# Grouped attention: the probabilities times values product in three terms of rounded and low parts, with x parked in DRAM

## The reference, cut to what matters

```
h   = layernorm(x) then rmsnorm, scaled by ln1          # 4 x 256 x 256
q   = rope(h @ Wq)     32 heads of 128                    # 4 key/value heads,
k   = rope(h @ Wk)      4 heads of 128                    # each for 8 query heads
v   = h @ Wv            4 heads of 128
p   = softmax(q k^T / sqrt(128), causal)
res = layernorm(x) + (p v) @ Wo
```

## Time and profile before

| what | value |
|---|---|
| median of 3 runs | 1535.27 us (1535.23 to 1543.98) |
| the profiled execution | 1537.94 us, span 1536.2 us |
| PE busy | 1342.8 us (87%) |
| PE weight loads | 987.4 us (64%) |
| DVE busy | 961.9 us (63%) |
| ACT busy | 792.4 us (52%) |
| POOL busy | 617.7 us (40%) |
| stage of the change | 716 to 1233 us of the span |
| rounds of its loop | 750 to 1232 us |

### The profile page before, as it was taken

How to read it: one execution, slowest core, us unless ns; L and a number is a source line. 1 busy time by engine, 2 the same in 40 slices (tenths; PEclk the granted TensorE clock), 3 DMA queues, 4 the chain that set the end, 5 groups by cost and what they waited for, 6 DMA issues and landing times. The chain is left out here.

```text
span 1536.2 us, 23871 instructions
## 1 busy us (share of the span) xinstructions
PE 1342.8 (87%) x8621; PEld 987.4 (64%) x8621; DVE 961.9 (63%) x1625; ACT 792.4 (52%) x1590; POOL 617.7 (40%) x550
## 2 busy tenths in 40 slices
PE   5788678899799579886789999999999869999998
PEld 4564455644388434433557777776777658888887
DVE  4763754558755587873677777877787554333443
ACT  2455104345532246664567777777877544445442
POOL 5110001101054511211566666666676445555553
PEclk8999779989999678996899999999999979999999
DMA  2000400020000100002000000000000023233231
GB/s 70 1 1 2 121 3 0 4 101 0 1 1 1 38 1 2 2 2 81 7 14 15 15 25 19 15 22 22 15 22 8 8 87 121 96 119 110 105 119 51
DMA packets 29492, 55.58 MB, mean 36 GB/s; under 512 B 6506, under 2 KB 16170, under 8 KB 29204
## 3 DMA queue, kind: packets, MB, share of 16 engines
q1 hardware_dynamic: 29396, 54.30, 11.0%
HBM read 52.98 MB, written 1.21 MB: 35 GB/s over the span
## 5 line engine op out<-in xcount | busy, mean ns | idle before, releaser
L2606 DVE TENSOR_TENSOR e_act<-e_gated,ps 128x512 f32<-128x512 f32 x66 | 45.4, 688 | 158.1 <-POOL e_gated L2411 158.1
L1839 POOL TENSOR_TENSOR a_raw<-a_prod 128x512 f32<-128x512 f32 x72 | 98.3, 1366 | 51.7 <-DVE a_prod L2243 51.7
L1844 POOL TENSOR_TENSOR a_q_low<-a_raw,a_q_high 128x512 fp32r<-128x512 f32 x64 | 82.8, 1294 | 87.2 <-ACT a_q_high L2103 87.2
L2240 DVE TENSOR_TENSOR a_prod<-ps,a_rot 128x512 f32<-128x512 f32 x72 | 49.7, 691 | 93.9 <-PE ps L1888 93.7
L2411 POOL TENSOR_TENSOR e_gated<-e_gate,e_wb 128x512 f32<-128x512 f32 x66 | 85.2, 1292 | 49.8 <-ACT e_gate L2532 44.5
L1848 POOL TENSOR_TENSOR a_o_low<-a_o,a_o_high 128x512 fp32r<-128x512 f32 x64 | 82.9, 1295 | 41.7 <-ACT a_o_high L2154 39.7
L2111 ACT ACTIVATE a_shift<-ident,a_nmax 128x128 bf16<-128x128 f32 x256 | 81.9, 390 | 32.3 <-DVE a_nmax L2252 32.0
L2402 POOL TENSOR_TENSOR e_we_low<-e_we,e_we_high 128x768 fp32r<-128x768 f32 x33 | 60.8, 1842 | 89.5 <-ACT e_we_high L2537 85.5
L1606 DVE SCALAR_TENSOR_TENSOR m_acc<-ps,m_conv_w,m_acc 128x1020 f32<-128x1020 f32 (+2 forms) x60 | 76.0, 1275 | 31.3 <-ACT m_acc L1526 29.9
L1360 PE MATMUL ps<-m_ln_T,m_win 128*128 128x512 f32 x192 | 88.8, 618 | 4.2 <-DMA m_win<-in_m_winT 3.5
L601 DVE TENSOR_REDUCE x_nmax<-ps 128x2 bf16<-128x512 f32 x128 | 82.5, 689 | 11.2 <-PE ps L371 10.9
(11 more groups left out here) (431 smaller groups left out, 4271.2 us busy)
## 6 DMA issues: line engine op xcount, KB each, us to landing
e_wb<-token_weights SPq DMA_DIRECT2D x32, 512.0 KB, 3.9
e_we<-in_experts SPq DMA_DIRECT2D x33, 384.0 KB, 3.1
a_wq<-in_a_wq SPq DMA_DIRECT2D x16, 256.0 KB, 2.7
a_wo<-in_a_wo SPq DMA_DIRECT2D x16, 256.0 KB, 2.8
m_win<-in_m_winT SPq DMA_DIRECT2D x2, 1024.0 KB, 8.8
nf_pickU<-in_nf_pickU SPq DMA_DIRECT2D x2, 768.0 KB
nf_raw<-in_ffn_w SPq DMA_DIRECT2D x3, 352.0 KB
x<-in_x SPq DMA_DIRECT2D x4, 256.0 KB, 6.6
```

What stands on the lines that cost most here:

```text
L1839: e.tensor_tensor(raw[:, i % 2, :], prod[:, i % 2, 0, :], prod[:, i % 2, 1, :], ALU.add).then_inc(s_raw, 1)
L1844: e.tensor_tensor(low_part, raw[:, i % 2, :], high_part.bitcast(F32), ALU.subtract).then_inc(s_xl, 1)
```

## The change

v is kept as a rounded part `vH` and a low part `vL`, the probabilities as `pH` and `pL`. Their product is vH pH + vH pL + vL pH, three fp32r matmuls for each one in fp32. The new work of a round: ACT `prob_high(n-1)` behind `exps(n-1)` rounds 128x768 probabilities in one instruction; POOL `prob_low` subtracts the long part, 128x512, behind `low`; DVE `prob_low` subtracts the short part, 128x256, behind `rotate` and ahead of `split`. In the prologue DVE makes eight `v_low` (128x512, one operand in PSUM) among the rotations.

To make room, buffers share memory: `raw` becomes the first half of `prod` (so `rotate(i)` waits until `low(i-2)` is done, where it waited for `add(i-2)`), the q pieces have three slots of 512 columns, the probabilities three (four before) beside four of pH and pL, `o_high` three (four before), wk, wv, the parts of wv, `pick32` and `normed` lie in buffers that are used later, and `inv`, `inv_high` and `o` lie in `core.x`. For that x is stored to DRAM (1 MB, the issue comes behind `odd` on SP) and DVE waits for that ahead of the loop; in the next stage SP loads it back behind the bias and ahead of experts 1 to 3, and POOL waits for it ahead of its x + res.

```diff
+        probT = sb("probT", [P, 3, 3 * S])
+        room = core.x[:].rearrange("p t d -> p (t d)")
+        inv, invH = (room[:, z:z + 2 * S].rearrange("p (r n) -> p r n", r=2) for z in (0, 2 * S))
+        o = room[:, 4 * S:8 * S].rearrange("p (r n) -> p r n", r=2)
+        pH, pL = sb("prob_high", [P, 4, 3 * S], F32R), sb("prob_low", [P, 4, 3 * S], F32R)
-        v = sb("v", [P, NT, NKV * P])
+        vH, vL = sb("v_high", [P, NT, NKV * P], F32R), sb("v_low", [P, NT, NKV * P], F32R)
         prod = sb("prod", [P, 2, 2, BANK])
-        raw = sb("raw", [P, 2, BANK])
+        raw = prod[:, :, 0, :]
...
             e.dma_start(odd[:], d["odd"]).then_inc(s_pick, 16)
+            e.dma_start(d["x_saved"], core.x[:].rearrange("p t d -> p (t d)")).then_inc(s_saved, 16)
...
+        def prob_low(e, n, part, done):
+            e.wait_ge(s_ph, n + 1)
+            e.tensor_tensor(pL[:, n % 4, part], probT[:, n % 3, part], pH[:, n % 4, part].bitcast(F32),
+                            ALU.subtract).then_inc(done, 1)
...  (POOL's loop)
                 for i in of_step.get(n - 1, ()):
                     low(e, i)
+                if 0 <= n - 1 < N:
+                    prob_low(e, n - 1, slice(0, 2 * S), s_pll)
...  (TensorE: values_of waits for v_low, values)
                 if t >= 4:
-                    e.wait_ge(s_vc, t - 3)
+                    e.wait_ge(s_vl, t - 3)
...
+                e.wait_ge(s_pll, s + 1)
+                e.wait_ge(s_pls, s + 1)
                 if s >= 1:
                     e.wait_ge(s_o, s)
-                e.matmul(out, v[:, 2 * b, g * P:(g + 1) * P],
-                         probT[:, s % 4, 0:2 * S].rearrange("p (h q) -> p h q", h=2), start=True, stop=False)
-                e.matmul(out[:, :, P:S], v[:, 2 * b + 1, g * P:(g + 1) * P],
-                         probT[:, s % 4, 2 * S:3 * S].rearrange("p (h q) -> p h q", h=2),
-                         start=False, stop=True).then_inc(s_av, 1)
+                for k, o, part in ((0, out, slice(0, 2 * S)), (1, out[:, :, P:S], slice(2 * S, 3 * S))):
+                    for i, (w, x) in enumerate(((vH, pH), (vH, pL), (vL, pH))):
+                        mm = e.matmul(o, w[:, 2 * b + k, group], heads(x[:, s % 4, part]), start=(k == i == 0),
+                                      stop=(k == 1 and i == 2))
+                mm.then_inc(s_av, 1)
...  (ACT's loop, behind exps(n - 1) and ahead of copy_spread)
+            def prob_high(n):
+                e.wait_ge(s_ex, 2 * n + 2)
+                if n >= 4:
+                    e.wait_ge(s_av, n - 3)
+                e.activation(pH[:, n % 4, :], probT[:, n % 3, :], ACT.Copy).then_inc(s_ph, 1)
...  (DVE)
+            def v_low(t):
+                e.wait_ge(s_vc, t + 1)
+                e.tensor_tensor(vL[:, t, :], ps[:, (P2_LONG, AV, SPREAD, OUT)[t % 4], :], vH[:, t, :].bitcast(F32),
+                                ALU.subtract).then_inc(s_vl, 1)
...
             def rotate(i):
                 e.wait_ge(s_pc, i + 1)
                 if i >= 2:
-                    e.wait_ge(s_raw, i - 1)
+                    e.wait_ge(s_xh, i - 1)
+                    e.wait_ge(s_xl, i - 1)
...
-            for i in range(1, FIRST):
-                rotate(i)
+            rotate(1)
+            rotate(2)
+            for t in range(4):
+                v_low(t)
+            rotate(3)
+            rotate(4)
+            for t in range(4, 6):
+                v_low(t)
+            rotate(5)
+            for t in range(6, 8):
+                v_low(t)
...  (DVE's loop)
                 for i in of_step.get(n, ()):
                     rotate(i)
+                if 0 <= n - 1 < N:
+                    prob_low(e, n - 1, slice(2 * S, 3 * S), s_pls)
                 if n % 2 and 0 <= n - 3 < N:
                     split((n - 3) // 2)
...  (next stage, SP and POOL)
             e.dma_start(bias[:], d["expert_bias"].partition_broadcast(P)).then_inc(s_w, 16)
+            e.dma_start(core.x[:].rearrange("p t d -> p (t d)"), d["x_saved"]).then_inc(s_back, 16)
...
             weights_low(0, 0)
+            e.wait_ge(s_back, 16)
             e.tensor_tensor(core.x[:], core.x[:], res[:], ALU.add).then_inc(s_xr, 1)
```

More of the change, by code:

```diff
@@ L1730, in stage_attention_1 @@
         mv, rstd1, rstd2, ahead = core.mv, core.rstd, core.rstd2, Ahead(core, "a1", res, "rms")
-        normed = sb("normed", [P, 4, D])
         hH, hL = sb("h_high", [P, KD, T], F32R), sb("h_low", [P, KD, T], F32R)
         over = sb("over", [P, 2, 2 * S])
-        o = sb("o", [P, 2, 2 * S])
-        wk, wv = over, o
-        wkH, wvH = sb("wk_high", [P, KD, NKV * P], F32R), sb("wv_high", [P, KD, NKV * P], F32R)
+        probT = sb("probT", [P, 3, 3 * S])
+        begin = probT[:].rearrange("p r n -> p (r n)")
+        wk, wv = (begin[:, z:z + KD * NKV * P].rearrange("p (k n) -> p k n", k=KD) for z in (0, 1024))
+        room = core.x[:].rearrange("p t d -> p (t d)")
+        inv, invH = (room[:, z:z + 2 * S].rearrange("p (r n) -> p r n", r=2) for z in (0, 2 * S))
+        invH = invH.bitcast(F32R)
+        o = room[:, 4 * S:8 * S].rearrange("p (r n) -> p r n", r=2)
+        pH, pL = sb("prob_high", [P, 4, 3 * S], F32R), sb("prob_low", [P, 4, 3 * S], F32R)
+        early = pH[:].rearrange("p r n -> p (r n)")
+        wvH, wvL = (early[:, z:z + KD * NKV * P].rearrange("p (k n) -> p k n", k=KD) for z in (1024, 2048))
+        wkH = sb("wk_high", [P, KD, NKV * P], F32R)
         wq, wqH = sb("wq", [P, 2, 2, KD, P]), sb("wq_high", [P, 2, 2, KD, P], F32R)
         wo, woH = sb("wo", [P, 2, 2, D]), sb("wo_high", [P, 2, 2, D], F32R)
-        wkL, wvL = sb("wk_low", [P, KD, NKV * P], F32R), sb("wv_low", [P, KD, NKV * P], F32R)
+        wkL = sb("wk_low", [P, KD, NKV * P], F32R)
         wqL, woL = sb("wq_low", [P, 2, 2, KD, P], F32R), sb("wo_low", [P, 2, 2, D], F32R)
@@ L1743, in stage_attention_1 @@
         ones = sb("ones", [P, 32])
-        pick32, pick = sb("pick32", [P, 4, P]), sb("pick", [P, 4, P], F32R)
+        pick32, pick = over[:, 0].rearrange("p (c n) -> p c n", c=4), sb("pick", [P, 4, P], F32R)
         odd = sb("odd", [P, 1])
@@ L1771, in stage_attention_1 @@
         s_p2, s_ex = sem("scores"), sem("probs")
+        s_ph, s_pll, s_pls = sem("probs_high"), sem("probs_low_long"), sem("probs_low_short")
+        s_vl, s_saved = sem("v_low"), sem("x_saved")
         s_sum, s_inv, s_ih, s_is = sem("sums"), sem("inverses"), sem("inverses_high"), sem("inverses_split")
@@ L1816, in target @@
             _, p, half, j = what
-            a = slice(half * BANK, (half + 1) * BANK)
-            return qH[:, p % 2, j, a], qL[:, p % 2, j, a], 2 * (B * (p - 2) + 2 * half + 2)
+            at = 2 * p + half
+            return qH[:, at % 3, j, :], qL[:, at % 3, j, :], 2 * (B * ((at - 3) // 2) + 2 * ((at - 3) % 2) + 2)
         def const_low(e, n):
@@ L1947, in first_scores @@
                 e.wait_ge(s_m1, n + 1)
-                a = b * S
+                a, at, z = b * S, (2 * p + b // 2) % 3, b % 2 * S
                 long = ps[:, P1_LONG, :].rearrange("p (h k) -> p h k", h=2)
                 for j in range(2):
-                    e.matmul(long[:, j, :], qH[:, p % 2, j, a + P:a + S], kH[:, p // 4 % 2, a:a + S],
+                    e.matmul(long[:, j, :], qH[:, at, j, z + P:z + S], kH[:, p // 4 % 2, a:a + S],
                              start=False, stop=True, skip_group_check=True)
@@ L1954, in first_scores @@
                 for j in range(2):
-                    e.matmul(short[:, j, :], qH[:, p % 2, j, a:a + P], kH[:, p // 4 % 2, a:a + P],
+                    e.matmul(short[:, j, :], qH[:, at, j, z:z + P], kH[:, p // 4 % 2, a:a + P],
                              start=(j == 0), stop=False, skip_group_check=True)
@@ L1970, in scores @@
                 keys = [w[:, g, a:a + P] for w in (kH, kL)]
-                both = [w[:, p % 2, :, a:a + S] for w in (qH, qL)]
+                both = [w[:, at, :, z:z + S] for w in (qH, qL)]
                 e.wait_ge(s_m2, 2 * n + 1)
@@ L1978, in scores @@
                 keys = [w[:, g, a + P:a + S] for w in (kH, kL)]
-                both = [w[:, p % 2, :, a + P:a + S] for w in (qH, qL)]
+                both = [w[:, at, :, z + P:z + S] for w in (qH, qL)]
                 e.wait_ge(s_m2, 2 * n + 2)
@@ L2095, in v_copy @@
                 e.wait_ge(s_v, t + 1)
-                e.activation(v[:, t, :], ps[:, (P2_LONG, AV, SPREAD, OUT)[t % 4], :], ACT.Copy).then_inc(s_vc, 1)
+                e.activation(vH[:, t, :], ps[:, (P2_LONG, AV, SPREAD, OUT)[t % 4], :], ACT.Copy).then_inc(s_vc, 1)
             def high(i):
@@ L2130, in exps @@
                 e.wait_ge(s_p2, 2 * n + 1)
-                if n >= 4:
-                    e.wait_ge(s_av, n - 3)
-                e.activation(probT[:, n % 4, 0:2 * S], ps[:, P2_LONG, :], ACT.Exp).then_inc(s_ex, 1)
+                if n >= 3:
+                    e.wait_ge(s_pll, n - 2)
+                    e.wait_ge(s_pls, n - 2)
+                    e.wait_ge(s_sum, (n - 3) // 2 + 1)
```

(6 more changed lines are left out.)

24 lines of the change are left out of this document (13 added, 11 removed).

## The result

The changed kernel takes **1607.65 us** (median of 4 runs, 1601.09 to 1613.08); the kernel before took 1536.48 on the same chip (1535.23 to 1543.98). The ratio is 1.045, 95% interval 1.0399 to 1.0501. The forecast was 1590, its range 1546 to 1625, its sign slower. The profiled execution took 1612.2 (span 1610.4), 74.3 more than the one before.

The account below looks back on a forecast made before the run. TensorE sets the pace now, DVE just behind; after the change the chain through DVE and ACT, plus the port, binds. 34 + 16 + 1 + 7 - 3 = +55 on 1537.94 gives 1593, 1590 as median; range 1546 to 1625.

Parts of the forecast that it names:

- its sign slower: Whole kernel: slower by over 1%, chance 0.79; within 1% 0.16, faster 0.05.
- 34 + 16 + 1 + 7 - 3 = 55: Collision in 24 pairs 34 us, six k-piece pairs 16, two last pairs 1, prologue 7, less 3 for splits already held.
- the gain: TensorE's values in the loop: 1.03 us instead of 1.29, 0.26 a round, 17 us over 64, counted inside pair times.
- the mask among the rivals: Rival: ACT's late second mask holds short scores, or POOL first; 1634 at most; above 1625, clock included, 0.08.
- its chain: Loop, divide to next divide through DVE and ACT, with prob_high and prob_low: 6.40 us in even rounds, 6.80 in odd.
- The collision, the step of +1.4 a pair: Odd rounds: split held 1.05 us by POOL's prob_low; pair 14.9, 34 us over 24 pairs; case 1568 to 1625, chance 0.63.
- two branches: Odd rounds: DVE first, split held, pair +1.4 (chosen); or POOL first, prob_low held too, pair +2.7.
- k pieces, +2.7: Six loop pairs with a k piece: rotate waits 1.6 for low, +2.7 each, 16 us in all, range 10 to 26.
- The prologue, +7: Ahead of the loop: eight v_low on DVE make the loop's first piece late, +7 us, between 5 and 10.
- Costed at nothing: x's transfer to DRAM and back, the slots of q, probabilities and o_high, and values' new waits: 0 us.
- The clock, a rival: Clock falls as TensorE idles more: +45 for a tenth of the loop, 1635; above 1625, either cause, chance 0.08.
- TensorE's gain survives, a rival: Loop pair 13.02: 1525 with prologue paid, chance 0.08; 1518 with it hidden, 0.04.

Follow-up runs that it names:

- fill: Changed kernel plus four more fp32r matmuls of 512 columns in even rounds while TensorE waits for split: 1592.84 us, ratio 1.0274; repeated on another chip 1596.47 us, 1.0381.
- after_again: The changed kernel itself, nothing altered, run once more in the third set of runs: 1607.07 us, ratio 1.0451 to the kernel before.
- no_lows: Changed kernel with both prob_low (DVE's and POOL's) left out, prob_high kept, TensorE's work the same: 1563.85 us, ratio 1.020 to the kernel before.
- terms_only: Changed kernel without prob_high and both prob_low; only the three matmuls, v_low and shared buffers are left: 1538.88 us, ratio 1.0033 to the kernel before.
- dve_early: Changed kernel, all arithmetic kept, DVE's prob_low moved a round later and ahead of the rotation: 1555.84 us, ratio 1.006 to the kernel before.
- no_v_low: Changed kernel without the prologue's eight v_low, rounded v standing in the third term: 1593.88 us, ratio 1.0375 to the kernel before.

## Why the prediction was right, and where not

**Sign and size.** The sum was 34 + 16 + 1 + 7 - 3 = 55. With the clock held up (`fill`), the loop is 497.4 against 449.2: +48.2, where the terms gave 34 + 16 + 1 - 3 = 48. The prologue is +8.3 to the first `maxima` where 7 was put. The clock makes +14.2 in the profiled execution (511.6 - 497.4), and 8.3 + 48.2 + 14.2 - 0.2 = 70.5. The forecast for this execution was 1593, and it took 1612: 14 of the 19 are the clock, for which the sum had no term, 4 the stages ahead, 1 the prologue.

**TensorE.** `values` is now 1.06 in the array (from 1022.70, its first slot in the next even round, to the piece at 1023.76), forecast 1.03. That the gain would be inside the pair times held for TensorE's own rounds: in `after_again` `values` start at 924.24, 931.29 and 939.67, so 7.05 for the one with `sums` (forecast 7.06) and 8.38 for the other (7.85).

**ACT.** 836 ns, as forecast. Its place costs more than was seen: 0.77 a pair by `no_lows` against `terms_only`, through the second mask and through `inverse_high`, which both come behind it. The forecast had the mask among the rivals only, and `inverse_high` nowhere: its chain followed the input of `prob_low`, not that of `split`, though the earlier trace rows had shown the case: there `split` waited 0.72 for `inverse_high` and then took 1.53. Here both lie beneath the larger delay of the odd rounds and show where that is taken away (`dve_early`).

**The collision, the step of +1.4 a pair.** Its size was nearly right at full clock: 15.13 against the 13.54 from which it was worked out, +1.59, and with the give-back, which lies in the mean of 13.70, +1.43. That is in good part luck. The forecast had two branches and chose one. If `prob_high` comes last, `prob_low` runs free and only `split` is held: 14.9 forecast, 14.5 measured, in five of the 20 pairs (seven with the extra matmuls). If the rotation comes last, POOL is first and both are held: 13.54 + 2.7 = 16.2 forecast, 15.45 measured at full clock, in fifteen (thirteen). "ACT's signal normally comes last on DVE" failed, then, in thirteen to fifteen of the 20 pairs: in the round shown `prob_high` ended at 1010.25 and the rotation at 1010.48. Both branches cost less than they were priced at, 1.0 and 1.9 instead of 1.4 and 2.7, and the mean of the two kinds happens to lie near the forecast's one. In the first kind `prob_low` takes 1.38 to 1.43 in most rounds at full clock and `split` 1.48, together up to 2.0 more than free; in the second only `split` is held, by 0.57 (1.05).

The story of what holds `split` fits only the second kind. Leaving POOL's `prob_low` out does not help, the pair is 15.16: another POOL instruction takes its place. What decides is that DVE's `prob_low` stands between the rotation and `split`; moving it alone takes the pair to 14.04 (`dve_early`).

The Trainium skill (SBUF, Who interferes with whom) says that the two block each other for the whole instruction. The trace agrees in both directions: the held DVE instruction ends 0.3 after POOL's, and where `split` wins, POOL's `add` takes 1.58 instead of 1.28.

**k pieces, +2.7.** The wait is there (1.65 on `low`, forecast 1.6), but more of it overlaps with the chain than was taken: 19.5 - 17.8 = +1.7 at full clock, near the lower bound. Five such pairs make 5 less than forecast, twenty others 4 more (20 x 0.19), the last four rounds 1.5 more (2.5 for 1). So the 48 came out almost exactly, by errors that cancel.

**The prologue, +7.** 5.2 for the first piece, 8.3 for the first `maxima`; `residual_of` is 4.56 now, not 5.61; why was not tested. `no_v_low` shows that `v_low` is all of it.

**Costed at nothing.** x's way out is right: it takes

```profile
x_saved<-x SPq DMA_DIRECT2D x1, 1024.0 KB, 7.9
```

and lies under the prologue. Back it makes x + res late, as forecast, and nobody waits.

**The clock, a rival.** It was priced at +45 for a tenth of the loop and given 0.08 together with another cause, for the reason that at 24.90 busy of 30 us the clock had been 1.00. That reason failed: the stretch from 950 to 1000 has 42.76 of 50, as high a share, and 0.90. The price was too high as well: a pair with such a stretch is 1.1 longer (16.5 against 15.45), or 2.0 where the same pair takes 14.5 with the extra matmuls, and one with a k piece 1.4 (20.9 against 19.5). In the first profile the loop stands at the lower clock for 56.0 us, in `fill` for 13.5; these 42.5 us, a twelfth of the loop, cost 14.2. `fill` shows it as a cause: `split` is held as long as in the changed kernel (1365 and 1374 ns), TensorE has more work, and the loop is shorter.

**TensorE's gain survives, a rival.** It mostly doesn't, even without the new work on ACT, DVE and POOL (`terms_only`): `split` loses to POOL's `add` in nine of the 20 pairs instead of three. What makes it lose more often stays open.

## What to carry to other kernels

Look at what stands on DVE behind an instruction that also releases POOL, when both read SBUF there. Directly behind it the DVE instruction won in 17 of the 20 odd rounds before the change and in 11 of 20 in `terms_only`. Anything that comes later in that place, because another instruction was put ahead of it or because its own input comes late, was held here until 0.3 after POOL's instruction, by up to 1.1 us. So before putting a cheap elementwise instruction there, look at what it pushes out, on ACT as well, and put it where its input is old and nobody is just released: here that took the ratio from 1.045 to 1.006 (on two chips) and the loop from 511.6 to 458.5, with the same work. A stall of TensorE is charged twice when the granted clock falls behind it, so a forecast that adds such stalls needs a term for it; here stalls of 1.24 us in most odd rounds brought 12 to 14 us.
